# Gated cross-attention blocks: the products of value and output weights kept in DRAM for the second half of the batch

## The reference

```python
q_hk = (hidden_q @ Wq.T).reshape(Bv, Sv, H, K)              # 16 heads of 128
q_big = jnp.einsum('bshk,hkq->bshq', q_hk, w_kc_q)          # 384 wide, then rope
q_r = jnp.einsum('bshq,hqr->bhsr', q_big, W_qr)
k_r = jnp.einsum('bld,hdr->bhlr', kv_r, W_kr)
scores = jnp.einsum('bhsr,bhlr->bhsl', q_r, k_r)
attn = jax.nn.softmax(scores, axis=-1)
ctx_c = jnp.einsum('bhsl,bld->bhsd', attn, kv_r)
ctx_lat = jnp.einsum('bhsd,hkd->bhsk', ctx_c, w_kc_kv)
ctx = ctx_lat.transpose(0, 2, 1, 3).reshape(Bv, Sv, H * K)
return ctx @ Wo.T
```

## Time and profile before

| | us |
|---|---|
| median of 3 runs | 2117.43 |
| lowest, highest | 2115.23, 2124.33 |
| the profiled execution | 2123.64 |
| its span, first to last instruction | 2121.9 |
| first stage (the one with the change) | about 0 to 1020 |
| TensorE busy over the span | 1877.3 |

### The profile page before, as it was taken

The page is one execution under the profiler, slowest core; times in us unless marked ns, Lnnn a source line. Parts: engine busy times, 40 slices in busy tenths (PEclk is TensorE's granted clock), DMA queues, the critical chain, the costliest instruction groups (busy, mean ns, idle before and its releaser), DMA issues. The chain is left out here.

```text
span 2121.9 us, 31624 instructions
## 1 busy us (share of the span) xinstructions
PE 1877.3 (88%) x11466; PEld 1489.5 (70%) x11466; DVE 1428.5 (67%) x2714; ACT 944.4 (45%) x1971; POOL 669.6 (32%) x620
## 2 busy tenths in 40 slices
PE   4899999999999999999427998899868899999997
PEld 4677778877678877777314554666545789999996
DVE  5777776778776777776677777477645535666664
ACT  3433333444433344433483332555425236666663
POOL 4322222226421222221113000232222464555553
PEclk9999999999999999999758999899978999999999
DMA  4111001110101110100321000000022347777774
GB/s 194 37 37 37 7 31 37 37 37 31 67 6 37 37 37 37 37 1 1 159 90 59 0 0 0 1 1 2 1 76 100 103 87 209 238 237 234 235 234 87
DMA packets 31106, 153.59 MB, mean 72 GB/s; under 512 B 5468, under 2 KB 5468, under 8 KB 20084
## 3 DMA queue, kind: packets, MB, share of 16 engines
q1 hardware_dynamic: 19268, 128.33, 16.6%
q0 software_dynamic: 11408, 23.37, 6.0%
q10 hardware_dynamic: 288, 0.00, 0.0%
HBM read 131.17 MB, written 20.51 MB: 71 GB/s over the span
## 5 line engine op out<-in xcount | busy, mean ns | idle before, releaser
L263 POOL TENSOR_TENSOR la_q_roped<-la_q_roped 128x400 f32<-128x400 f32 x128 | 132.6, 1056 | 668.4 <-DVE la_q_roped L683 668.4
L588 ACT ACTIVATE la_probs<-banks,la_minus_max 100x361 f32<-100x361 f32 x256 | 144.5, 564 | 196.5 <-DVE la_minus_max L736 196.5
L683 DVE TENSOR_TENSOR la_q_roped<-banks,la_rope_q 128x400 f32<-128x400 f32 x384 | 196.8, 566 | 30.9 <-PE banks L386 15.1
L1877 DVE TENSOR_TENSOR ex_weights_low<-ex_raw_weights,ex_weights_high 128x2048 fp32r<-128x2048 f32 x60 | 137.6, 2294 | 51.4 <-ACT ex_weights_high L1772 48.8
L423 PEld LDWEIGHTS banks<-identity,la_probs 100*121 100x121 f32 x768 | 113.1, 184 | 70.8 <-DVE la_probs L743 44.7
L743 DVE TENSOR_SCALAR la_probs<-la_probs,la_rsum 100x361 f32<-100x361 f32 x256 | 154.1, 602 | 9.1
L1030 PE MATMUL banks<-qf_sign_weights,qf_x_quant_t 128*100 128x512 bf16 x512 | 122.2, 389 | 33.0 <-DVE qf_hidden L1111 18.6
L434 PE MATMUL banks<-la_probs_t,la_kv_rows 121*128 121x200 f32 x768 | 151.3, 332 | 0.0
L736 DVE TENSOR_REDUCE la_minus_max<-banks 100x1 f32<-100x361 f32 x256 | 135.0, 527 | 16.2 <-PE banks L414 9.6
L423 PE MATMUL banks<-identity,la_probs 100*121 100x100 f32 x768 | 126.0, 273 | 21.2 <-DVE la_probs L743 18.3
L2144 POOL TENSOR_TENSOR ex_g_low<-ex_g,ex_g_high 128x256 fp32r<-128x256 f32 (+1 forms) x104 | 86.5, 948 | 180.9 <-ACT ex_g_high L1816 180.5
(11 more groups left out here) (321 smaller groups left out, 5370.7 us busy)
## 6 DMA issues: line engine op xcount, KB each, us to landing
ex_raw_weights<-w_exp SPq DMA_DIRECT2D x60, 1024.0 KB, 4.9
la_weights<-w_pack SPq DMA_DIRECT2D x15, 1856.0 KB, 7.6
qf_raw_weights<-w_ffn SPq DMA_DIRECT2D x2, 4096.0 KB, 22.0
residual<-x SPq DMA_DIRECT2D x2, 2048.0 KB, 14.7
qf_raw_weights<-w_ffn SPq DMA_DIRECT2D x2, 2048.0 KB
out<-ex_block_out POOLq DMA_DIRECT2D x13, 256.0 KB, 4.0
normed_rows<-ex_xn SPq DMA_DIRECT2D x16, 200.0 KB
out<-residual SPq DMA_DIRECT2D x4, 800.0 KB
```

The source lines that it names most:

```text
L263: pool.tensor_tensor(roped[:, h, 0, c, :], roped[:, h, 0, c, :], roped[:, h, 1, 1 - c, :], ALU.add).then_inc(b_add, 1)
L588: act.activation(prob[:, s % 4, 0:L], ps[0:S, s % 2, 0:L], ACT.Exp, bias=nmax[:, s % 4:s % 4 + 1], accum_out=sums[:, s % 4:s % 4 + 1]).the ...
L683: dve.tensor_tensor(roped[:, h, v, c, :].rearrange("p (b s) -> p b s", b=GB), ps[:, B_BANKS[k % 2], 0:NT].rearrange("p (b s) -> p b s", b=GB),
L1877: dve.tensor_tensor(wl[:, m, :], raw[:, m, :], wh[:, m, :].bitcast(F32), ALU.subtract).then_inc(w_low[m], 1)
```

## The change

For passes 0 to 7 the high and low part of the products are stored in a DRAM tensor by SP's queue, once both parts are there. In passes 8 to 15 TensorE's two products, ScalarE's two evictions and VectorE's two subtractions are left out; Pool's queue loads the parts of the same pair from DRAM into the same tiles, behind the split and, in pass 8, the rotation, and ahead of partners. The first output product of such a pass waits for that load. wout_high waits for the stores of the passes before, since it overwrites what they read.

```diff
+    kept_m = nc.dram_tensor("wout_parts", (PAIRS, 2, DC, 2 * D), F32).ap()
...
+        m_out, m_in = sem("wout_stored"), sem("wout_loaded")
...
                 sp.dma_start(wts[1][:], w_pack[1]).then_inc(w_in[1], 16)
+
+                def keep(n):
+                    sp.wait_ge(m_low, 2 * n + 2)
+                    for i, m in enumerate((mh, ml)):
+                        sp.dma_start(kept_m[n, i], m[:].rearrange("p h d -> p (h d)").bitcast(F32)).then_inc(m_out, 16)
+
                 for n in range(2, RUNS):
+                    if n <= PAIRS + 1:
+                        keep(n - 2)
                     sp.wait_ge(k_psum, (n - 1) * UNITS)
...
+                def bring(n):
+                    pool.wait_ge(m_out, 32 * PAIRS)
+                    pool.wait_ge(o_psum, n * HB)
+                    for i, m in enumerate((mh, ml)):
+                        pool.dma_start(m[:].rearrange("p h d -> p (h d)"),
+                                       kept_m[n - PAIRS, i].bitcast(F32R)).then_inc(m_in, 16)
+
...
                     if starts_half(n):
                         rotate(1, range(HB))
+                    if n >= PAIRS:
+                        bring(n)
                     for u in range(UNITS):
                         partners(n, u)
...
                     if b >= 1:
                         pe.wait_ge(v_low, n * HB + b)
-                    else:
+                    elif n < PAIRS:
                         pe.wait_ge(m_low, n * 2 + 1)
...
-                    if b == 0:
+                    if b == 0 and n < PAIRS:
                         pe.wait_ge(m_low, n * 2 + 2)
+                    elif b == 0:
+                        pe.wait_ge(m_in, 32 * (n - PAIRS + 1))
                     else:
                         pe.wait_ge(o_add, n * HB + b)
...
-                    wout(n, 0)
+                    if n < PAIRS:
+                        wout(n, 0)
                     absorb(n, 0)
                     widen(n, 3, 0)
-                    wout(n, 1)
+                    if n < PAIRS:
+                        wout(n, 1)
...
                 def wout_high(n, h):
                     act.wait_ge(m_psum, n * 2 + h + 1)
+                    if n:
+                        act.wait_ge(m_out, 32 * n)
...
                     qk_high(n, 0)
-                    wout_high(n, 0)
+                    if n < PAIRS:
+                        wout_high(n, 0)
...
-                        if s == 0:
+                        if s == 0 and n < PAIRS:
                             wout_high(n, 1)
...
-                        if s in (MIX - 2, MIX - 1):
+                        if s in (MIX - 2, MIX - 1) and n < PAIRS:
                             wout_low(n, s - MIX + 2)
```

## The result

The changed kernel took 2111.28 us in the median of 13 runs (2106.13 to 2115.53), the kernel before, in 13 runs, 2121.85 us (2115.23 to 2126.24). The ratio is 0.9958, with a 95% interval of 0.9944 to 0.9972: 8.9 us faster by this ratio, between 5.9 and 11.9; the two medians lie 10.6 apart. The forecast of 10.9 us is 0.9949 of the median it started from, and lies inside.

What follows compares the result with a forecast made beforehand. TensorE, 88% busy, was taken as the bound. Late passes save 0.93 + 0.5 = 1.43 us: 7 x 1.43 + 0.93 = 10.9 us off the 2117.43 median, giving 2106.5 us, range 2101 to 2115.

Steps and rivals of the forecast that it cites:

- First product: TensorE, line 404 ahead of absorb: without it absorb starts at 622.83 instead of 623.76, 0.93 us a late pass.
- Second product, evictions, second subtraction: TensorE's 0.87 us beside VectorE's chain, ScalarE's two evictions (557), VectorE's later subtraction held by Pool's split: each gains nothing.
- longer wait at the first transposes: Sign on TensorE before line 423: the wait grows by 0.5 us or more, since the second product's time turns into it.
- First subtraction: VectorE, line 701 ahead of slot 4's maximum: second absorb comes sooner, bounds 0.36 and 0.66, taken as 0.5 us.
- Pool's loads: Two loads on Pool's queue ahead of partners: 2.04 us of issue within 4.9 us free, so they cost nothing.
- The slower rival: Pool's issue makes partners late and narrow wait; at 5 us each, 30 us lost, 2147 us; chance 0.07.
- Stores: Early passes, two 512 KB stores on SP's queue ahead of the weight load: nothing, upper bound perhaps 0.1 us a pass.
- only the first product: Rival: Pool's split still holds absorb in slot 5, so 8 x 0.93 = 7.4 us, 2110.0 us; chance 0.17.
- TensorE's whole time: Rival: all of both products' 0.95 + 0.87 us come back, 14.6 us, 2102.9 us; chance 0.13.

Runs made afterwards that it cites:

- the one with 16 issues: The changed kernel with each of the two Pool loads of passes 8 to 15 cut by columns into eight, 16 issues ahead of partners: 2155.68 us.

## Why the prediction was right

**First product: right, and measured.** Predicted 0.93 us, 0.86 by putting it back. The difference is the start behind the rank copy: the copy ended at 621.93 and absorb started 0.15 us later, where 0.06 was taken from the second absorb.

**Second product, evictions, second subtraction: right, nothing.** Each was put back alone and left the late pitch within 0.02 us. But the time of the second product did not turn into a longer wait at the first transposes, as the prediction said. That wait is 0.80 us as before; the product's time went into two waits ahead of it, 0.45 us for qk_low, which the prediction had not named, and 0.33 instead of 0.15 for the exponential.

**First subtraction: right, 0.42 for 0.5**, nearer the row's 0.36 than the upper bound of 0.66. This term was too large by 0.08 us and the first product's by 0.07, which makes 1.27 us a pass in place of 1.43. Pass 8 (1.49) and pass 15 (0.87 for 0.93) complete 10.0 us of stage in place of 10.9. The ratio's 8.9 us lies 1.1 from that, well inside its interval. The absolute time of 2111.28 us is inside 2101 to 2115, but 4.8 above the forecast of 2106.5. Of this, 4.4 are the starting point: the kernel before had 2117.43 in its first three runs and 2121.85 in thirteen. With the same gain a few microseconds more of that would have left the range.

**Pool's loads: right.** Two issues of 0.56 us instead of 1.02, partners undisturbed, narrow's wait 0.2 us. The nearest row was less near than it was called: line 2105 is no plain store, the kernel has it add to what lies in DRAM (accum_op=ALU.add). The free time was 4.3 to 4.4 us, not 4.9: the first issue starts 0.5 us after the modelled end of the last output matmul, and 2.20 us (609.88 to 612.08) and 2.15 us are left. 4.3 us cost nothing, 8.6 us cost a pass over 5. The slower rival had the right place and mechanism, and its price would have been higher than worked out, since the clock falls too: 8.6 us less 4.9 is 3.7, where passes grew by 5.4 to 5.7. That no tensor_scalar runs where Pool issues them, so that nothing stretches the issues, held too: 0.54 to 0.76 us in all 16.

**Stores: right, nothing.** Early pitch 60.79 against 60.78. (1 MB at the rate of 1856 KB in 7.6 us is 4.2 us, not the 4.3 of the text; nothing hangs on it.)

**Against the rivals:** "only the first product" would have left a pitch of 59.9, "TensorE's whole time" 59.0; 59.51 lies between, at the forecast's 59.35. The total alone (8.9 us, between 5.9 and 11.9) speaks against the second (14.6 us), but could not tell the forecast (10.9) from the first (7.4); that took the pitch. The ratio fell just on the near side of the 0.5% line that the forecast lay beyond.

## What to carry to other kernels

Removing work from the busiest engine pays only where the next thing that engine does was ready: look at each removed instruction's place, find what its successor waits for, and price it by that wait, not by its duration. Twins in one pass, 2.5 us apart, were worth 0.86 us and nothing. When the gain is a fraction of a per cent, measure it in the trace by the pitch of a repeated pass, which repeats to 0.03 us where whole executions spread by 9, and look at the clock of the passes compared.

## What the runs showed of the hardware that was not expected

A wait of 4.2 us on TensorE in an otherwise full stage lowered the granted clock from 1.00 to 0.50 in every pass that had it, and narrow behind it took 1.4 to 2.2 us longer. Shorter waits can do it too, but not every time: behind 1.25 us in pass 8, shortly after one of 0.35 us, the clock fell in six of twelve executions. Waits of up to 0.8 us, several in a pass, left it at 1.00 in passes 1 to 6 and 9 to 14 of all kernels but the one with 16 issues.

Pool's issue of a load took 0.54 and 0.56 us (medians) for 512 KB and 0.56 to 0.63 us for a quarter or an eighth of that, so for these loads of 128 rows it goes by the transfer. The Trainium skill (SBUF — State Buffer, "Who interferes with whom") says that a VectorE operation in a two-port mode and one of GpSimd exclude each other for a whole instruction. VectorE's side of it is seen here: the tensor_scalars take 0.41 us with Pool idle and up to 1.90 us when they meet its split of 1.6 to 2.4 us, each ending 0.2 us after the operation that it met; with the split moved away they are at 0.41.
